# Query/key stage of a local attention: the cosine product from PSUM on VectorE, sine product and sum on GpSimd, values shifted by tile, the last norms in two parts

## The chip, the cores and the metric

The kernel runs on one core of a Trainium2 chip. The metric is the device time of one execution in microseconds (us), and the reported value is the median over runs.

## What is computed

The input x has 4 batches of 1024 tokens with 128 features. It is normalised per token, and two branches work on the result: a small attention block with a feed-forward layer (called A here), and two layers of a windowed attention with a gated feed-forward layer (B). Both are added to x. The change lies in branch B, in what stands between the projection and the attention of each layer:

```python
def _layer(x, wqkv, qs, ksc, wo, lg, lb, w1, b1, w2, b2):
    h = shift_token(x)
    q, k, v = jnp.split(h @ wqkv, 3, axis=-1)      # 8 heads of 64
    ...
    q = l2norm(q) * qs
    k = l2norm(k) * ksc
    q = q * cos * scale + rotate_half(q) * sin * scale
    k = k * cos / scale + rotate_half(k) * sin / scale
    o = local_attention(q, k, v)                   # windows of 64, each looks at itself and the one before
    x = x + o @ wo
    ...
```

The norm is a factor per head and token, so the kernel rotates first and puts the factor in later: for keys by a multiplication, for queries as the scale of the exponential.

## The kernel before, in words

One loop over the four batches holds one program per engine. The order on each engine is the order in which its function is written, and the engines meet at counting semaphores. All of q and k is kept transposed, features on partitions: 8 tiles of 128 features (two heads each), in two chunks of 512 tokens, so 16 tiles of 128x512 per layer. In each chunk k = 0 to 3 are the keys, 4 to 7 the queries. Four PSUM banks form a ring for all products (`product`, L510); a product waits for `drained`, the bank's release by its last reader.

The stage around the change, per tile:
- TensorE makes the product (L510) in a ring bank.
- ScalarE copies it with the q or k scale into `raw` (L976, four slots) and its square into `sq` (L980), which releases the bank.
- SP sends two DMAs that exchange rows of `raw` pairwise into `rot` (L452, four slots).
- VectorE makes `pc` = raw x cosine table (L1038) and `ps_` = rot x sine table (L1040), two buffers each (`rotate`).
- GpSimd adds them into `qk` (L494). VectorE's next use of a buffer waits for the sum two tiles before.

After four tiles TensorE sums the squares over the heads (`sum_squares`, L739). After the 8 tiles of a chunk come four value products, which ScalarE copies into `vB` (L995); the sums of squares are copied (L990) and transposed (`turn_sums`, L747), and VectorE takes the inverse root of them in small steps (`norms`, L292 to L297) and splits those of the keys into three bf16 parts (L1176 to L1179). The parts are transposed (L755), copied (L965) and spread over the partitions by a product; VectorE multiplies the keys by them (`scale`, L1188). The norms of chunk 0 are taken at the start of chunk 1, those of chunk 1 after its last tile. In layer 0 ScalarE also has the logarithm and exponential of branch A's layer norm there (`ln_root`, L921 and L926), right after chunk 0.

The values are needed shifted by 64 tokens as well: SP copies each chunk of `vB` with two DMAs into `vS` (L460, L462) once all its four tiles are there.

The window attention then takes 8 tiles of 128 queries: mask (L620) and scores (L628), maxima (L1085), exponentials by ScalarE (L872), their scaling by VectorE (L1103) and GpSimd (L500), transposes (L640), products with the values (L656). ScalarE's and VectorE's functions for it are called `window_attention` too.

## Time and profile before

| What | Value |
|---|---|
| Median of 3 runs | 1446.84 us (1443.94 to 1450.88) |
| The profiled execution, its own time | 1459.8 us |
| Span in that profile | 1458.1 us |
| Mean granted TensorE clock | 0.877 |
| Busy: TensorE, VectorE, ScalarE, GpSimd | 1124.0, 878.6, 768.9, 291.5 us |
| GpSimd sums `qk<-pc,ps_` (L494) | 128 of 1518 ns mean |
| Sine products `ps_<-rot,tab_s` (L1040) | 128 of 1347 ns mean |
| Cosine products `pc<-raw,tab_s` (L1038) | 128 of 854 ns mean |

The span is the time from the first to the last instruction of the profiled execution; the execution's own time has what lies around it. A mean mixes steps that ran alone with steps that had to wait for another engine inside their own duration, so single rows of the time line say more than the means here.

### The profile page before, as it was taken

Reading aid. Unit: us, or ns where it says so; the run is one execution under the profiler, and the core shown is the slowest. Engines: PE = TensorE matmul, PEld = TensorE weight load, DVE = VectorE, ACT = ScalarE, POOL = GpSimd, SP = SyncE. Lnnn points to the kernel's source line nnn. Section 1 sums busy time; section 2 is a strip of 40 time slices with the busy share of each in tenths; the row PEclk is TensorE's granted clock in tenths of the full one; section 3 lists DMA queues with packets and bytes.
Section 4 is the critical chain, followed back from the end, with each engine's and each line's share of the span. In section 5 each row is a group of like instructions: output and inputs, shape, how many; then the busy total and the mean of one; then the engine's idle time right before and its main releaser. Section 6 shows DMA issues by size and latency. Waiting matters only on the chain. (4 is left out here: it accounts for less than half of the span.)

```text
span 1458.1 us, 23509 instructions
## 1 busy us (share of the span) xinstructions
PE 1124.0 (77%) x8682; PEld 620.1 (43%) x8754; DVE 878.6 (60%) x1738; ACT 768.9 (53%) x1928; POOL 291.5 (20%) x228
## 2 busy tenths in 40 slices
PE   5986788678698668867869877886787976797677
PEld 4752453154374245325437425432534732542353
DVE  5549655963445865596345596468545467648744
ACT  1355674485235556447523556653942453945574
POOL 1105112410101411241010141033202033204210
PEclk9698899889859879988986988997997796999799
DMA  6003101400101310140010131023001014003100
GB/s 260 1 29 117 27 1 58 112 2 15 31 1 45 101 27 1 58 112 2 15 32 1 51 98 23 1 73 98 2 15 32 1 59 111 2 1 123 48 16 15
DMA packets 39201, 66.22 MB, mean 45 GB/s; under 512 B 5408, under 2 KB 19232, under 8 KB 37152
## 3 DMA queue, kind: packets, MB, share of 16 engines
q1 hardware_dynamic: 37920, 62.43, 14.0%
q10 hardware_dynamic: 1152, 2.10, 0.4%
q8 instruction: 78, 1.28, 0.4%
q14 instruction: 51, 0.42, 0.1%
HBM read 13.12 MB, written 2.10 MB: 10 GB/s over the span
## 5 line engine op out<-in xcount | busy, mean ns | idle before, releaser
L494 POOL TENSOR_TENSOR qk<-pc,ps_ 128x512 f32<-128x512 f32 x128 | 194.3, 1518 | 583.8 <-DVE ps_ L1040 583.8
L872 ACT ACTIVATE prob<-bank,negb,inv_norm 128x128 f32<-128x128 f32 x512 | 233.0, 580 | 57.3 <-DVE negb L1087 57.3
L1040 DVE TENSOR_TENSOR ps_<-rot,tab_s 128x512 f32<-128x512 f32 x128 | 172.5, 1347 | 25.9 <-DMA rot<-raw 25.9
L872 ACT ACTIVATION_READ_ACCUMULATOR prob<-bank,negb,inv_norm 128x1 f32 x512 | 163.3, 328 | 0.0
L510 PE MATMUL bank<-hTz,wb_s 128*128 128x512 f32 x256 | 139.5, 675 | 4.3 <-ACT sq L980 4.3
L1085 DVE TENSOR_REDUCE negb<-bank 128x8 f32<-128x1024 f32 x64 | 78.3, 1223 | 94.5 <-PE bank L628 94.4
L976 ACT ACTIVATE raw<-bank,vec_s 128x512 f32<-128x512 f32 x128 | 90.0, 703 | 81.6 <-PE bank L510 46.5
L500 POOL TENSOR_TENSOR prob<-prob,recb 128x512 f32<-128x512 f32 x64 | 66.7, 1041 | 320.1 <-DVE recb L1107 320.1
L1038 DVE TENSOR_TENSOR pc<-raw,tab_s 128x512 f32<-128x512 f32 x128 | 109.3, 854 | 18.2 <-ACT raw L976 18.1
L656 PE MATMUL bank<-probT,vS 128*64 128x64 f32 x1024 | 67.9, 231 | 38.6 <-issue 34.2
L510 PE MATMUL bank<-hTz,w_s 128*128 128x512 f32 (+1 forms) x192 | 87.8, 602 | 12.2 <-DVE hTz L1127 12.2
L620 PE MATMUL bank<-cbf_s 128*128 128x512 bf16 x80 | 35.7, 485 | 71.8 <-ACT prob L872 56.0
L980 ACT ACTIVATE sq<-bank 128x512 f32<-128x512 f32 x128 | 77.8, 608 | 24.1 <-PE bank L739 24.1
L536 PEld LDWEIGHTS bank<-kD,qZ 32*128 32x128 f32 x1024 | 81.7, 245 | 20.2 <-issue 20.2
L841 ACT ACTIVATE a_probT<-bank 128x512 f32<-128x512 f32 x64 | 38.1, 596 | 92.9 <-PE bank L547 92.9
L536 PE MATMUL bank<-kD,qZ 32*128 32x64 f32 (+1 forms) x1024 | 86.9, 335 | 0.0
L628 PE MATMUL bank<-qk 64*64 64x128 f32 (+1 forms) x2048 | 86.5, 311 | 0.0
L628 PEld LDWEIGHTS bank<-qk 64*64 64x64 f32 x2048 | 68.5, 158 | 37.0 <-issue 37.0
L1051 DVE TENSOR_REDUCE a_max<-bank 128x8 f32<-128x512 f32 x64 | 43.9, 686 | 64.5 <-PE bank L536 64.5
L510 PE MATMUL bank<-wb_s,hTz 128*128 128x512 f32 x128 | 75.6, 693 | 3.6 <-ACT sq L980 3.4
L510 PEld LDWEIGHTS bank<-hTz,wb_s 128*128 128x128 f32 x256 | 49.5, 208 | 65.6 <-issue 58.0
L656 PEld LDWEIGHTS bank<-probT,vS 128*64 128x64 f32 x1024 | 55.7, 140 | 50.8 <-issue 42.9
(151 smaller groups left out, 2020.8 us busy)
## 6 DMA issues: line engine op xcount, KB each, us to landing
rot<-raw SPq DMA_DIRECT2D x256, 128.0 KB, 2.0
vS<-vB SPq DMA_DIRECT2D x24, 512.0 KB, 4.4
vS<-vB SPq DMA_DIRECT2D x8, 384.0 KB, 5.7
xn_tok<-x SPq DMA_DIRECT2D x5, 512.0 KB, 3.6
tab_s<-tabs SPq DMA_DIRECT2D x1, 2048.0 KB, 21.0
vS<-x SPq DMA_DIRECT2D x4, 512.0 KB, 3.7
out<-vS SPq DMA_DIRECT2D x8, 256.0 KB, 2.4
wb_s<-wb SPq DMA_DIRECT2D x1, 1536.0 KB, 16.6
```

The costliest lines, as they stand in the source:

```text
L494: pool.tensor_tensor(dst, pc[:, j % 2, :], ps_[:, j % 2, :], ALU.add).then_inc(sum_rdy, 1)
L500: pool.tensor_tensor(p, p, wide(recb[:, t % 2, 1, :]), ALU.mult).then_inc(win_norm[1], 1)
L510: mm = pe.matmul(bank[0:m, i % RING, 0:n], lhs, rhs, start=(q == 0), stop=(q == len(parts) - 1))
L536: mm = pe.matmul(bank[:, m % 4, n0:(w + 1) * 2 * A_WIN], qZ[r, q0 // A_WIN, :, :].rearrange("p j q -> p (j q)"), kD[r, k0:q0 + A_WIN], sta ...
L628: mm = pe.matmul(dst[64 * half:64 * half + 64, g, (h + 1) * P - w:(h + 1) * P], qk[r, h, q0:q0 + 64], qk[r, 4 + h, q0 + 64 - w:q0 + 64], s ...
L656: mm = pe.matmul(head_bank[t % 2][64 * g:64 * g + 64, h * P + 64 * half:h * P + 64 * half + 64], v, probT[:, t % 2, g, h, 64 * half:64 * h ...
L872: ins = act.activation(prob[:, t % 2, g, h, :], s_bank[t % 2][:, g, h * P:(h + 1) * P], ACT.Exp, bias=negb[:, t % 2, g, h:h + 1], scale=qu ...
L976: act.activation(raw[:, jb % 4, :], bank[:, i % RING, :], ACT.Identity, scale=vec_s[:, g:g + 1]).then_inc(raw_rdy, 1)
L980: act.activation(sq[:, jb % 4, :], bank[:, i % RING, :], ACT.Square)\
L1038: dve.tensor_tensor(pc[:, j % 2, :], raw[:, jb % 4, :], ct, ALU.mult)
L1040: dve.tensor_tensor(ps_[:, j % 2, :], rot[:, jb % 4, :], st, ALU.mult).then_inc(prod_rdy, 1)
L1085: link(dve.tensor_reduce(b_, s_bank[t % 2].rearrange("p g (h k) -> p g h k", h=4), AX_X, ALU.max, negate=True))
```

## The change

- VectorE makes the cosine product straight from the product's PSUM bank, the q or k scale included, in one instruction after ScalarE has made the square, and this releases the bank.
- GpSimd makes the sine product (`exchanged`) and the sum. The product of a tile is issued ahead of the sum of the tile before it.
- ScalarE's copy into `raw` waits for the exchange that last read the slot. A new semaphore `squared` says that a square is there.
- The sums of squares of chunk 1 are turned in two parts, keys (n = 1) and queries (n = 2); the norms of the queries of chunk 1 are taken inside the attention, ahead of the third tile's maxima.
- The values are shifted tile by tile in chunk 1, tiles 0 to 3 behind the exchanges of its first four tiles, tiles 4 to 7 at its end; each tile has its own semaphore.
- The scores of the tiles 0 to 3 wait for the sums of chunk 0, those of the tiles 4 to 7 for chunk 1; `prob` lies over `sq`, and `probT` over `raw`, so the first copy into `probT` waits for the last sum.

```diff
-        with nc.sbuf_tensor("prob", [P, 2, 2, 4, P], F32) as prob, nc.sbuf_tensor("probT", [P, 2, 2, 4, P], F32) as probT:
+        with nc.sbuf_tensor("probT", [P, 2, 2, 4, P], F32) as probT:
             pass
         raw = sb("raw", [P, 4, CH])
         rot = sb("rot", [P, 4, CH])
...
+        with nc.sbuf_tensor("prob", [P, 2, 2, 4, P], F32) as prob:
+            pass
         sq = sb("sq", [P, 4, CH])
...
                             sp.wait_ge(prod_rdy, jb - 3)
                         for r in range(2):
                             sp.dma_start(rot[r::2, slot, :], raw[1 - r::2, slot, :]).then_inc(rot_rdy[slot], 16)
-                        if jb % B_QK == B_QK - 1:
...
+                        if jb // B_QK % CHUNKS:
+                            k = jb % B_QK
+                            for t in range(TPC, TILES) if k == B_QK - 1 else (k,) if k < TPC else ():
                                 taken(sp, values_use(l, t))
-                            if l:
-                                sp.wait_ge(win_heads, on(l, 0))
-                            t0, t1 = c * TPC, (c + 1) * TPC
-                            sp.dma_start(vS[64:128, t0:t1, :], vB[0:64, t0:t1, :]).then_inc(v_shifted, 16)
-                            u1 = min(t1, TILES - 1)
-                            sp.dma_start(vS[0:64, t0 + 1:u1 + 1, :], vB[64:128, t0:u1, :]).then_inc(v_shifted, 16)
+                                if t == TPC:
+                                    sp.wait_ge(sums_turned, 3 * l + 3)
+                                if l:
+                                    sp.wait_ge(win_heads, on(l, 0))
+                                sp.dma_start(vS[64:128, t, :], vB[0:64, t, :]).then_inc(v_shifted[t], 16)
+                                if t + 1 < TILES:
+                                    sp.dma_start(vS[0:64, t + 1, :], vB[64:128, t, :]).then_inc(v_shifted[t + 1], 16)
...
                 def _(pool):
+                    def exchanged(l, c, k):
...
+                        j = pair(l, c, k)
+                        jb = j - 4
+                        pool.wait_ge(rot_rdy[jb % 4], 32 * (jb // 4 + 1))
+                        pool.wait_ge(sum_rdy, j - 1)
+                        pool.tensor_tensor(ps_[:, j % 2, :], rot[:, jb % 4, :],
+                                           tab_s[:, 3 if k < 4 else 1, cc(c)], ALU.mult).then_inc(prod_rdy, 1)
...
-                                else:
-                                    pool.wait_ge(prod_rdy, j - 4 + 1)
-                                    dst = qk[:, qk_tile(k), cc(c)]
...
+                                    pool.tensor_tensor(dst, pc[:, j % 2, :], ps_[:, j % 2, :],
...
+                                if c == 0 and k == 0:
...
+                                        pool.wait_ge(mm_full, USE0["a_wo"] + 4)
+                                        pool.wait_ge(tab_b_in, 16)
+                                    exchanged(br, 0, 0)
+                                if k + 1 < B_QK or c + 1 < CHUNKS:
+                                    exchanged(br, c + (k + 1) // B_QK, (k + 1) % B_QK)
+                                pool.wait_ge(prod_rdy, j - 4 + 1)
+                                taken(pool, qk_use(br, c, k))
+                                pool.tensor_tensor(qk[:, qk_tile(k), cc(c)], pc[:, j % 2, :], ps_[:, j % 2, :],
                                                    ALU.add).then_inc(sum_rdy, 1)
...
+                        if t % TPC == 0:
+                            pe.wait_ge(sum_rdy, pair(l, t // TPC, B_QK - 1) + 1)
...
-                        pe.wait_ge(v_shifted, 32 * (l * CHUNKS + t // TPC + 1))
+                        pe.wait_ge(v_shifted[t], (32 if t else 16) * (l + 1))
...
                                 k = 4 * part + m
-                                taken(pe, qk_use(l, c, k))
-                                mm = pe.matmul(bank[32 * m:32 * m + 32, 4 + c, :], sum_s[:, part, :], sq[:, m, :],
...
+                                pe.wait_ge(squared, pair(l, c, k) - 3)
+                                alone = c == 1
+                                mm = pe.matmul(bank[32 * m:32 * m + 32, 4 + (c and not part), :], sum_s[:, part, :],
+                                               sq[:, m, :], start=(alone or part == 0), stop=(alone or part == 1),
+                                               skip_group_check=True)
                             mm.then_inc(ss_done, 1)
...
-                        def turn_sums(c):
...
+                            pe.wait_ge(sums_copied, l * 3 + n + 1)
...
-                                if tt == 0:
+                                if c == 0 and tt == 0:
                                     sum_squares(c, 1)
-                                if tt == 1:
-                                    turn_sums(c)
+                                if c == 0 and tt == 1:
+                                    turn_sums(0)
+                                if c and tt == 0:
+                                    turn_sums(1)
+                                if c and tt == 1:
+                                    sum_squares(c, 1)
+                        turn_sums(2)
                         turn_norms(1)
...
-                                    act.wait_ge(prod_rdy, jb - 3)
...
-                                act.activation(sq[:, jb % 4, :], bank[:, i % RING, :], ACT.Square)\
-                                   .then_inc(drained[i % RING], 1)
+                                act.activation(sq[:, jb % 4, :], bank[:, i % RING, :], ACT.Square).then_inc(squared, 1)
                                 if c and k == 3:
...
+                            if c:
+                                copy_sums(1)
...
-                                if tt == 0:
-                                    act.wait_ge(ss_done, (l * CHUNKS + c + 1) * 2)
-                                    act.activation(ss[:, c, :], bank[:, 4 + c, :], ACT.Copy)\
-                                       .then_inc(sums_copied, 1)
+                                if c == 0 and tt == 0:
+                                    copy_sums(0)
+                                if c and tt == 2:
+                                    copy_sums(2)
...
-                            jb = j - 4
-                            dve.wait_ge(raw_rdy, RAW0[br] + c * 8 + k + 1)
-                            dve.tensor_tensor(pc[:, j % 2, :], raw[:, jb % 4, :], ct, ALU.mult)
-                            dve.wait_ge(rot_rdy[jb % 4], 32 * (jb // 4 + 1))
-                            dve.tensor_tensor(ps_[:, j % 2, :], rot[:, jb % 4, :], st, ALU.mult).then_inc(prod_rdy, 1)
+                            qs = V_L + br * VL_N + VL_QS + qk_tile(k) // 4
+                            dve.wait_ge(squared, j - 3)
+                            dve.scalar_tensor_tensor(pc[:, j % 2, :], bank[:, i % RING, :], vec_s[:, qs:qs + 1], ct,
+                                                     ALU.mult, ALU.mult).then_inc(drained[i % RING], 1)
...
+                        if t == 0:
+                            dve.wait_ge(sum_rdy, pair(l, 1, B_QK - 1) + 1)
...
-                    def window_attention(l):
...
                         for t in range(TILES):
+                            if t == 1:
+                                norms(2)
...
-                        def norms(c):
-
...
+                        def norms(n):
...
+                            dve.wait_ge(sums_turned, l * 3 + n + 1)
+                            c, e0, e1 = ((0, 0, 4), (1, 0, 2), (1, 2, 4))[n]
+                            y = inv_norm[:, c, :, :, e0:e1].rearrange("p t k e -> p (t k) e")
+                            inv_root(dve, link, bank[:, 4 + n, :].rearrange("p (t e) -> p t e", e=32)[:, :, e0:e1],
+                                     1e-24, ALU.max, 16 * (e1 - e0), y)
+                            if n == 2:
+                                return
...
-                        for k in range(4, B_QK):
-                            dve.wait_ge(sum_rdy, pair(l, 1, k) + 1)
                         scale(1, range(4))
-                        window_attention(l)
```

GpSimd's order at the start of the query/key stage of layer 0, before (`qk<-pc,ps_` is the sum, `prob<-prob,recb` the scaling in the attention, `rotary_products` the semaphore of the two products):

```order
L494 TENSOR_TENSOR qk<-pc,ps_ 128x512 [waits product_ready,rotary_products]
L494 TENSOR_TENSOR qk<-pc,ps_ 128x512 [waits rotary_products] x15
L500 TENSOR_TENSOR prob<-prob,recb 128x512 [waits window_sums_inverted] x8
```

and now, first the start of the stage, then its end (`rows_exchanged` is the exchange, `rotated` the sum's semaphore; the bank's release stands for the cosine product):

```order
L483 TENSOR_TENSOR ps_<-rot,tab_s 128x512 [waits rows_exchanged0,rotated,rotation_tables_b_loaded,product_ready]
L483 TENSOR_TENSOR ps_<-rot,tab_s 128x512 [waits rotated,rows_exchanged1]
L514 TENSOR_TENSOR qk<-pc,ps_ 128x512 [waits bank2_drained,rotary_products]
L483 TENSOR_TENSOR ps_<-rot,tab_s 128x512 [waits rotated,rows_exchanged2]
L514 TENSOR_TENSOR qk<-pc,ps_ 128x512 [waits bank3_drained,rotary_products]
L483 TENSOR_TENSOR ps_<-rot,tab_s 128x512 [waits rotated,rows_exchanged3]
L514 TENSOR_TENSOR qk<-pc,ps_ 128x512 [waits bank0_drained,rotary_products]
...
L483 TENSOR_TENSOR ps_<-rot,tab_s 128x512 [waits rotated,rows_exchanged3]
L514 TENSOR_TENSOR qk<-pc,ps_ 128x512 [waits bank0_drained,rotary_products]
L514 TENSOR_TENSOR qk<-pc,ps_ 128x512 [waits bank2_drained,rotary_products]
L520 TENSOR_TENSOR prob<-prob,recb 128x512 [waits window_sums_inverted] x8
```

GpSimd has two steps per tile in place of one, and the product for the next tile stands ahead of each sum.

VectorE's order in the attention of layer 0, from the scaling of the first tile to the maxima of the third, before:

```order
L1101 RECIPROCAL recb<-sumb 128x4 [waits window_probs_ready]
L1103 TENSOR_TENSOR prob<-prob,recb 128x512 [waits vector_step]
L1107 RECIPROCAL recb<-sumb 128x4 [waits window_probs_ready]
L1085 TENSOR_REDUCE negb<-bank 128x8 [waits window_probs_ready,window_scores_ready]
L1087 TENSOR_TENSOR negb<-negb,inv_norm 128x8 [waits vector_step]
```

and now:

```order
L1139 RECIPROCAL recb<-sumb 128x4 [waits window_probs_ready]
L1141 TENSOR_TENSOR prob<-prob,recb 128x512 [waits vector_step]
L1145 RECIPROCAL recb<-sumb 128x4 [waits window_probs_ready]
L295 TENSOR_SCALAR nw<-bank 128x32 [waits sums_of_squares_turned]
L296 TENSOR_SCALAR inv_norm<-nw 128x16x2 [waits vector_step]
L298 TENSOR_TENSOR nw<-inv_norm 128x32 [waits vector_step]
L299 SCALAR_TENSOR_TENSOR nw<-nw 128x32 [waits vector_step]
...
L300 SCALAR_TENSOR_TENSOR inv_norm<-nw,inv_norm 128x16x2 [waits vector_step]
L1121 TENSOR_REDUCE negb<-bank 128x8 [waits window_probs_ready,window_scores_ready,vector_step]
L1123 TENSOR_TENSOR negb<-negb,inv_norm 128x8 [waits vector_step]
```

The inverse root of the queries of chunk 1, eleven small steps of 128x32, has come in ahead of the third tile's maxima (L1121).

## Rows read from the trace of the kernel before

**Rows 1.** The page, part 1: busy time, share of the span, instructions of each engine.
```profile
PE 1124.0 (77%) x8682; PEld 620.1 (43%) x8754; DVE 878.6 (60%) x1738; ACT 768.9 (53%) x1928; POOL 291.5 (20%) x228
```

**Rows 2.** Time line, TensorE: first mask product of two window attentions; start us, length us, engine.
```profile
1236.81 0.63 PE L620 MATMUL bank<-cbf_s 128*128 128x512 bf16 x1 [1.87 <-DVE qk L1188]
...
1370.53 0.63 PE L620 MATMUL bank<-cbf_s 128*128 128x512 bf16 x1 [2.32 <-DVE qk L1188]
```

**Rows 3.** Time line, VectorE, layers 0 and 1 of the last batch.
```profile
1184.56 0.69 DVE L1040 TENSOR_TENSOR ps_<-rot,tab_s 128x512 f32<-128x512 f32 x1 [1.85 <-DMA rot<-raw]
...
1321.99 0.69 DVE L1040 TENSOR_TENSOR ps_<-rot,tab_s 128x512 f32<-128x512 f32 x1 [1.84 <-DMA rot<-raw]
1322.60 0.69 DVE L1038 TENSOR_TENSOR pc<-raw,tab_s 128x512 f32<-128x512 f32 x1
...
1327.17 0.68 DVE L1038 TENSOR_TENSOR pc<-raw,tab_s 128x512 f32<-128x512 f32 x1
1327.78 1.75 DVE L1040 TENSOR_TENSOR ps_<-rot,tab_s 128x512 f32<-128x512 f32 x1
```

**Rows 4.** Time line, GpSimd: set-up, first batch, layer 1 of the last batch.
```profile
0.75 0.52 POOL L345 MEMSET vS<- 64x512 f32 x1 [0.29 <-POOLq L1397]
1.21 0.09 POOL L346 MEMSET xT<- 128x1 f32 x1
...
27.04 1.81 POOL L473 MEMSET vS<- 128x2048 f32 x1 [25.64 <-POOLq L323]
28.90 0.49 POOL L476 MEMSET vS<- 64x64 f32 x2
35.48 1.27 POOL L494 TENSOR_TENSOR kD<-pc,ps_ 128x512 f32<-128x512 f32 x1 [6.09 <-DVE ps_ L1032]
...
1327.33 1.65 POOL L494 TENSOR_TENSOR qk<-pc,ps_ 128x512 f32<-128x512 f32 x1 [0.63 <-DVE ps_ L1040]
...
1361.34 1.27 POOL L494 TENSOR_TENSOR qk<-pc,ps_ 128x512 f32<-128x512 f32 x1 [1.23 <-DVE ps_ L1040]
1378.51 1.04 POOL L500 TENSOR_TENSOR prob<-prob,recb 128x512 f32<-128x512 f32 x1 [15.90 <-DVE recb L1107]
```

**Rows 5.** Time line, VectorE: steps that run beside a GpSimd step.
```profile
36.27 0.75 DVE L1032 SCALAR_TENSOR_TENSOR ps_<-bank,bias,tab_s 128x512 f32<-128x512 f32 x1
...
1351.20 0.68 DVE L1188 TENSOR_TENSOR qk<-bank,qk 128x512 f32<-128x512 f32 x1
1351.80 1.37 DVE L1038 TENSOR_TENSOR pc<-raw,tab_s 128x512 f32<-128x512 f32 x1
```

**Rows 6.** Time line, TensorE: six products at full clock, one at the lower.
```profile
1317.58 5.31 PE L510 MATMUL bank<-hTz,wb_s 128*128 128x512 f32 x12
...
1355.02 2.07 PE L510 MATMUL bank<-wb_s,hTz 128*128 128x512 f32 x2
```

**Rows 7.** Time line, ScalarE: logarithm, exponential (layer 0), first raw copy (layer 1).
```profile
1193.38 1.28 ACT L921 ACT_TABLE_LOAD   x1
...
1197.25 1.15 ACT L926 ACTIVATE oT<-oT 128x512 f32<-128x512 f32 x2
...
1318.64 0.69 ACT L976 ACTIVATE raw<-bank,vec_s 128x512 f32<-128x512 f32 x1 [4.82 <-PE bank L510]
```

**Rows 8.** Time line, VectorE: the last norms of layer 1.
```profile
1361.73 0.93 DVE L293 TENSOR_SCALAR inv_norm<-nw 128x64 int32<-128x64 int32 x1
1362.69 0.23 DVE L295 TENSOR_TENSOR nw<-inv_norm 128x64 f32<-128x64 f32 x1
...
1365.68 0.19 DVE L1179 TENSOR_TENSOR rsp<-nw,rsp 128x32 bf16<-128x32 f32 x1
```

**Rows 9.** Time line, VectorE: maxima of the third tile in the attention.
```profile
1381.29 1.22 DVE L1085 TENSOR_REDUCE negb<-bank 128x8 f32<-128x1024 f32 x1 [2.86 <-PE bank L628]
```

**Rows 10.** Windows: us, busy PE, PEld, DVE, ACT, POOL; then granted clock, DMA share, GB/s.
```profile
1354.00:1358.00 4.00, 3.48 (x11) 0.80 (x11) 4.00 (x5) 0.66 (x2) 2.38 (x2) 0.51 0.18 66
```

**Rows 11.** Time line, SP queue: one issue of a value shift.
```profile
1336.40 0.60 SPq L462 DMA_DIRECT2D vS<-vB  x1
```

More of the change, by code:

```diff
@@ L206, in program @@
         next_in = sem("next_x_loaded")
-        v_shifted = sem("values_shifted")
+        v_shifted = [sem(f"values_shifted{t}") for t in range(TILES)]
         win_scored = sem("window_scores_ready")
@@ L289, in inv_root @@
             if root is not None:
-                v, t, s = (z.rearrange("p (a e) -> p a e", e=4) for z in (v, t, s))
+                v, t, s = (z.rearrange("p (a e) -> p a e", e=root.shape[-1]) for z in (v, t, s))
                 y = root
@@ L880, in window_lay @@
                         act.wait_ge(win_turned, 2 * on(l, t) + 2)
+                        if t == 0:
+                            act.wait_ge(sum_rdy, pair(l, 1, B_QK - 1) + 1)
                         if on(l, t) >= 2:
@@ L962, in _, with copy_sums @@
                     for l in range(LAYERS):
+                        def copy_sums(n):
+                            act.wait_ge(ss_done, l * 4 + n + 2)
+                            act.activation(ss[:, n % 2, :], bank[:, 4 + n % 2, :], ACT.Copy).then_inc(sums_copied, 1)
                         def copy_norms(c):
@@ L1201, in _ @@
                         norms(1)
[L1202 to L1203 removed]
                         scale(1, range(4))
[L1205 removed]
+                        window_attention(l, norms)
                         for c in range(CHUNKS):
```

27 lines of the change are left out of this document (12 added, 15 removed).

## Prediction

> **What bounds the kernel now.** I read the page first, then the time lines of VectorE (DVE) and GpSimd (POOL) through the query/key stage, then that of ScalarE, and TensorE's clock by windows. The page names no single engine: TensorE is busy 77%, VectorE 60% [rows 1]. The change touches one stage, which runs eight times (four batches, two layers), so that stage is what must be read. I let it begin at the first sine product, which waits for the exchanged rows, and end at the first mask product of the window attention (PE L620): 1321.99 to 1370.53 us, 48.5 us, in layer 1 of the last batch, and 1184.56 to 1236.81, 52.3 us, in layer 0 [rows 2, 3].
>
> In it VectorE never rests: cosine product, sine product, next tile, and three tile starts lie 4.57 us apart, 2.28 a tile. But a sine product takes 1.75 us, and 0.69 where GpSimd is idle [rows 3]. The GpSimd sum beside it takes 1.65 us with VectorE's two-tensor products around it and 1.27 without [rows 4]. The two engines take turns whenever VectorE reads two SBUF tensors: the sine product really starts when the sum ends. What reads PSUM is free of this: a scaling step takes 0.68 us beside a sum, the two-tensor product right behind it stretches to 1.37, and the very form that the change brings (PSUM, a column, a table) took 0.75 us beside a sum of 1.27 [rows 4, 5].
>
> **What the change does to it.** VectorE keeps one product per tile, 0.75 us, instead of two; GpSimd gets the other beside its sum. VectorE's saving (1.5 us a tile) is worth nothing by itself once GpSimd is slower than it.
>
> *GpSimd's pair.* A step over three full SBUF tiles takes 1.27 us undisturbed; the only other GpSimd form of this size, with a broadcast operand, takes 1.04. A step that waits for its own engine's last result starts 0.05 us after its end; one that doesn't, 0.06 before it [rows 4]. A pair is 1.21 + 1.27 + 0.05 = 2.5 us, with bounds 2.1 (both at 1.04) and 2.6 (nothing hidden). I take 2.5, since the product reads two full tiles just as the sum does. The product is issued one tile ahead of its sum.
>
> *The path in layer 1*, from the same start: the first product 1.2, six pairs to the sum of tile 5: 16.2. Here the stage has a knot. There are two pc buffers, so tile 7's cosine product (0.75) waits for the sum of tile 5; its bank is what the fourth value product wants (0.9); then come tile 8's own product (0.9 [rows 6]), the raw copy 0.7, issue and exchange 2.7 (1319.33 to 1321.99 [rows 3, 7]) and three hops of 0.1: 22.4. GpSimd is out of work at 18.7 and waits 3.7 us. Before, VectorE filled this time with the first norms, so what is gained by an engine that has no norms to do is lost again. Then the sum of tile 7 comes at 24.9, seven more pairs end at 42.4, the last sum at 43.7.
>
> *The last norms* are next on VectorE after tile 15's cosine product, at 40.7, with three GpSimd steps still to run. All their small steps but the first read SBUF only: before, the second took 0.93 us instead of some 0.2, until the last sum (1361.34 + 1.27) was over [rows 4, 8]. Three are held so up to 43.7; eleven are left, at 0.245 each (13 of them lie between 1362.69 and 1365.87): 46.4. From there to the mask product it is 4.66 us as before [rows 2, 8]: 51.1. Against 48.5 that is **+2.5 us**.
>
> *Layer 0.* ScalarE's logarithm and exponential (5.0 us from 1193.38 on) stand ahead of the value copies [rows 7]. In the new order their input is ready at 12.9 and they end at 17.9, the copies run to 20.9, and tile 8's rows come at 24.3, 1.9 later than in layer 1. That makes 53.0 against 52.3: **+0.7**.
>
> *Norms inside the attention.* Eleven steps of 0.245, 2.7 us, plus up to 1.0 held by GpSimd's scaling at 1378.51 [rows 4], go into a gap of VectorE of 2.86 us [rows 9]. They make the third tile's maxima some 0.7 us late: +0.6 a stage (0 to 1.6).
>
> *Clock.* TensorE's granted clock was 0.51 (towards 1.2 GHz) in part of the second half, after stretches with little to do; a product took 2.07 us there, 0.89 at full clock (2.4 GHz) [rows 6, 10]. The knot has two products on the path. The bounds are 0 and +2.3, with another 1.1 at the end; I take +0.5, since before this place ran at full clock.
>
> *The rest.* Starting the scores on the first half's sums gains nothing while the norms of the second half's keys end last. The shifts by tile cost SP some 0.6 us an issue [rows 11]: four issues, 2.4 us a tile in four tiles, still under a pair. Tile 8's exchange no longer stands behind 1 MB of shifted values, but is late for other reasons. Probabilities that lie over the squares, and the raw copy's wait for the exchange instead of the product, cost nothing: both are over before.
>
> **Sum:** 4 x 2.5 + 4 x 0.7 + 8 x 0.6 + 8 x 0.5 = 21.6, +22 us. On the profiled execution (1459.8 us, some 13 above the median of the three runs) that is 1482; carried to the median of 1446.8 it is **1469 us**.
>
> A rule beside it. A lone step takes 1.27 us [rows 4]. The Trainium skill (GPSIMD Engine Reference, 3.1 Elementwise — side-by-side cycle accounting) gives about 2.6 cycles per element for a two-input step at 1.2 GHz, by estimate 1.11 us for 512, the rest being dispatch; with the dispatch hidden a pair would be 2.3 and the time that of rival 3. Its 4.1 Engine selection sends elementwise work to VectorE and so speaks against the change; the rows agree for a single step, 0.69 against 1.27 us.
>
> **Rivals.**
> (1) *GpSimd's pairs run at 2.1 us*, as the 1.04 bounds them. The knot is then at 19.8; four tiles behind it are paced by SP at 2.5, and the last sum comes at 39.2. Layer 1 gains 1.9 us, layer 0 3.7, less 1.1 for the last two terms: 8 x 1.7 = 14, **1433**. It decides from below 2.3 us a pair. For it: 1.27 is known of additions only. Against: the new step has no broadcast operand. 0.15.
> (2) *VectorE's small steps slip in* between and beside GpSimd's. The last norms end at 44.3, 2.1 earlier, and 22 - 17 is left: **1452**. Against it stand rows 8. 0.13.
> (3) *GpSimd hides its start-up* from step to step: a pair of 2.3 saves 0.2 on the 14 pairs of the path, 22 us in all: **1447**. The rows show 0.06 hidden and no more. 0.09.
> (4) *The clock stays low* from the knot on, as TensorE has one product to do in 2.5 us: both bounds of that term, 2.9 us more a stage: **1492**. Against: the density was hardly higher before. 0.13.
> The order of instructions shows that the change does what it says, so that it does nothing is no rival.
>
> **How the numbers follow.** The forecast has 0.50; alone it would range from 1456 to 1482 (pairs of 2.4 to 2.6, the norms' 0 to 1.6). A measurement can tell 0.5%, 7 us, from no change. Slower by more: 0.50 + 0.13 = 0.63; within it: 0.13 + 0.09 = 0.22; faster: 0.15. The range from 1430 to 1490 leaves out about half of (1) and of (4) and a little of the forecast.
>
> **What would show it.** Right: ps_<-rot,tab_s on GpSimd at 1.2 to 1.3 us and pairs 2.5 apart; one GpSimd wait of 3 to 6 us a stage, for an exchange, at tile 8; pc at 0.75 us from PSUM; steps of the last norms of about 1.2 us, three times a stage; a stage of 51 us in layer 1 and 53 in layer 0. Wrong: pairs under 2.3, last norms with all steps at 0.2, GpSimd waiting for pc, or a stage that begins or ends otherwise.

## The result, and the profile after

The changed kernel takes 1502.2 us (median of 4 runs, 1498.1 to 1505.5), the kernel before in the same session 1448.9 (4 runs, 1443.9 to 1459.5): ratio 1.036, interval 1.029 to 1.042. It is slower, as forecast, but by 53 us and not by 22, and it lies outside the range (1430 to 1490). In every comparison below, the ratio leaves out runs more than 1.5% above the fastest of their kernel, while the medians are over all runs.

The first rows are the page of the changed kernel: part 1, and the groups of part 5 for the sine product, the cosine product and the sum (busy time, mean ns of one, idle time ahead and its releaser).

```profile
PE 1172.0 (78%) x8714; PEld 636.7 (42%) x8786; DVE 746.4 (50%) x1698; ACT 773.0 (51%) x1936; POOL 417.6 (28%) x356
...
L483 POOL TENSOR_TENSOR ps_<-rot,tab_s 128x512 f32<-128x512 f32 x128 | 162.2, 1270 | 509.2 <-issue 188.4
...
L1075 DVE SCALAR_TENSOR_TENSOR pc<-bank,vec_s,tab_s 128x512 f32<-128x512 f32 x128 | 96.0, 750 | 239.0 <-POOL qk L514 190.9
...
L514 POOL TENSOR_TENSOR qk<-pc,ps_ 128x512 f32<-128x512 f32 x128 | 163.4, 1280 | 0.0
```

Against [rows 1], VectorE has lost 132 us of work and GpSimd has gained 126, and VectorE now stands idle 191 us for the sums of GpSimd. The step durations are those of the prediction: 1.27 and 0.75 us.

Next is the time line of GpSimd, layer 1 of the last batch, from the first products to the last sum (start us, length us, engine):

```profile
1361.27 2.51 POOL L483 TENSOR_TENSOR ps_<-rot,tab_s 128x512 f32<-128x512 f32 x2 [48.00 <-issue]
1363.74 1.27 POOL L514 TENSOR_TENSOR qk<-pc,ps_ 128x512 f32<-128x512 f32 x1
1365.15 1.27 POOL L483 TENSOR_TENSOR ps_<-rot,tab_s 128x512 f32<-128x512 f32 x1
1366.37 1.26 POOL L514 TENSOR_TENSOR qk<-pc,ps_ 128x512 f32<-128x512 f32 x1
1367.78 1.27 POOL L483 TENSOR_TENSOR ps_<-rot,tab_s 128x512 f32<-128x512 f32 x1
...
1384.36 1.27 POOL L483 TENSOR_TENSOR ps_<-rot,tab_s 128x512 f32<-128x512 f32 x1 [3.55 <-DMA rot<-raw]
...
1395.35 1.27 POOL L483 TENSOR_TENSOR ps_<-rot,tab_s 128x512 f32<-128x512 f32 x1 [0.61 <-DMA rot<-raw]
...
1398.13 1.28 POOL L483 TENSOR_TENSOR ps_<-rot,tab_s 128x512 f32<-128x512 f32 x1 [0.28 <-DMA rot<-raw]
...
1401.26 1.27 POOL L483 TENSOR_TENSOR ps_<-rot,tab_s 128x512 f32<-128x512 f32 x1 [0.63 <-DMA rot<-raw]
...
1404.18 1.27 POOL L483 TENSOR_TENSOR ps_<-rot,tab_s 128x512 f32<-128x512 f32 x1 [0.43 <-ACT vB L1032]
1405.41 2.50 POOL L514 TENSOR_TENSOR qk<-pc,ps_ 128x512 f32<-128x512 f32 x2
```

Three things are to be seen. A pair (product and sum, GpSimd's work for one tile) takes 2.63 us (1365.15 to 1367.78): the sum starts 1.22 behind its product, the next product 1.41 behind the sum. The knot, where GpSimd runs out of work, stands at the ninth tile, as forecast (3.55 us for an exchange). And four more waits follow, which the forecast didn't have. In the same place of layer 0 the knot is longer:

```profile
1242.32 1.26 POOL L483 TENSOR_TENSOR ps_<-rot,tab_s 128x512 f32<-128x512 f32 x1 [6.79 <-DMA rot<-raw]
```

By windows, TensorE's granted clock around the knot of layer 0 and in the second half of layer 1 (columns as in [rows 10], which has 0.51 over 4 us of the second half before; 0.5 is the level of 1.2 GHz):

```profile
1228.00:1236.00 8.00, 7.40 (x16) 2.06 (x17) 4.28 (x4) 4.46 (x8) 7.25 (x6) 0.55 0.01 2
...
1389.00:1405.00 16.00, 13.23 (x24) 3.90 (x25) 7.40 (x12) 5.10 (x9) 13.76 (x12) 0.50 0.38 116
```

The last norms of layer 1 came as forecast, three small steps held until GpSimd's last sum is over, and then free (to compare with [rows 8]):

```profile
1404.67 0.82 DVE L296 TENSOR_SCALAR inv_norm<-nw 128x32 int32<-128x32 int32 x1
1405.52 1.21 DVE L298 TENSOR_TENSOR nw<-inv_norm 128x32 f32<-128x32 f32 x1
1406.77 1.19 DVE L299 SCALAR_TENSOR_TENSOR nw<-nw 128x32 f32<-128x32 f32 x1
1407.99 0.19 DVE L300 SCALAR_TENSOR_TENSOR inv_norm<-nw,inv_norm 128x32 f32<-128x32 f32 x1
```

**Where the time went.** From the first sine product to the first mask product, as the prediction measures it, the eight stages take 407.0 us before and 443.6 after: +36.6, in layer 1 48.9 on average and +5.0 each, in layer 0 52.9 and +4.2 each. The attention behind them, from the first mask product to the end of the last product with the values, takes 354.8 and 359.8 (+5.0). The other 3.6 us of the 45.0 between the two profiled executions (1459.8 and 1504.8) lie ahead of the first stage, which begins at 106.1 us before and at 109.7 after. The change leaves that stretch alone, and it takes 100 to 110 us in the traces of this study, whatever the kernel. The step from 45 to the 53 of the medians is no work of the kernel: the profiled execution of before lay 11 us above its runs' median, that of after 3.

### The profile page after: what moved, and what is told of

The parts are those of the page before. It is cut to its first block and busy times, and to the rows that moved or that the text cites. A ratio compares the mean times of both kernels' runs of the same rounds, so it can differ in the third digit from the quotient of the medians.

```text
span 1503.1 us, 24013 instructions
## 1 busy us (share of the span) xinstructions
PE 1172.0 (78%) x8714; PEld 636.7 (42%) x8786; DVE 746.4 (50%) x1698; ACT 773.0 (51%) x1936; POOL 417.6 (28%) x356
## 5 line engine op out<-in xcount | busy, mean ns | idle before, releaser
L483 POOL TENSOR_TENSOR ps_<-rot,tab_s 128x512 f32<-128x512 f32 x128 | 162.2, 1270 | 509.2 <-issue 188.4
L1075 DVE SCALAR_TENSOR_TENSOR pc<-bank,vec_s,tab_s 128x512 f32<-128x512 f32 x128 | 96.0, 750 | 239.0 <-POOL qk L514 190.9
L530 PE MATMUL bank<-hTz,wb_s 128*128 128x512 f32 x256 | 156.6, 739 | 60.7 <-DVE pc L1075 60.6
L514 POOL TENSOR_TENSOR qk<-pc,ps_ 128x512 f32<-128x512 f32 x128 | 163.4, 1280 | 0.0
L1121 DVE TENSOR_REDUCE negb<-bank 128x8 f32<-128x1024 f32 x64 | 78.2, 1223 | 72.8 <-PE bank L650 72.5
L530 PE MATMUL bank<-wb_s,hTz 128*128 128x512 f32 x128 | 90.0, 807 | 12.4 <-DVE pc L1075 12.4
L662 PE MATMUL bank<-ident_s,prob 128*128 128x128 f32 x512 | 81.2, 307 | 0.5 <-POOL prob L520 0.2
L678 PEld LDWEIGHTS bank<-probT,vS 128*64 128x64 f32 x1024 | 56.9, 143 | 51.1 <-issue 42.2
```

The source lines that it names most:

```text
L483: pool.tensor_tensor(ps_[:, j % 2, :], rot[:, jb % 4, :], tab_s[:, 3 if k < 4 else 1, cc(c)], ALU.mult).then_inc(prod_rdy, 1)
L514: pool.tensor_tensor(qk[:, qk_tile(k), cc(c)], pc[:, j % 2, :], ps_[:, j % 2, :], ALU.add).then_inc(sum_rdy, 1)
L530: mm = pe.matmul(bank[0:m, i % RING, 0:n], lhs, rhs, start=(q == 0), stop=(q == len(parts) - 1))
L662: mm = pe.transpose(turn_bank[g][:, h * P:(h + 1) * P], prob[:, t % 2, g, h, :], ident_s[:, :])
L678: mm = pe.matmul(head_bank[t % 2][64 * g:64 * g + 64, h * P + 64 * half:h * P + 64 * half + 64], v, probT[:, t % 2, g, h, 64 * half:64 * h ...
L1075: dve.scalar_tensor_tensor(pc[:, j % 2, :], bank[:, i % RING, :], vec_s[:, qs:qs + 1], ct, ALU.mult, ALU.mult).then_inc(drained[i % RING], 1)
```

## The experiments

Below, "stage" runs from VectorE's first cosine product to the first mask product, in the last batch (layer 0, layer 1), since the sine product moves between engines: 54.8 and 51.1 us before, 59.4 and 56.0 in the changed kernel. Ratios are against the kernel before on the same chip. Its median there was 1452.2 us for experiments 1 to 4, 1453.7 for 5 to 8 and 1455.9 for 9 to 12 (1448.9 beside the changed kernel), so a difference in us between two groups is uncertain by some 5 us. Line numbers in rows are those of each experiment's own kernel. The experiments stand in the order of the argument, not of their numbers.

**1. The sine product goes back to VectorE.** On the changed kernel, in VectorE's rotate and (the lines taken out) in GpSimd's program:

```diff
-                    def exchanged(l, c, k):
...
-                                if k + 1 < B_QK or c + 1 < CHUNKS:
-                                    exchanged(br, c + (k + 1) // B_QK, (k + 1) % B_QK)
...
+                            jb = j - 4
+                            dve.wait_ge(rot_rdy[jb % 4], 32 * (jb // 4 + 1))
+                            dve.tensor_tensor(ps_[:, j % 2, :], rot[:, jb % 4, :], st, ALU.mult).then_inc(prod_rdy, 1)
```

> The changed kernel with the sine product back on VectorE (cosine product still from PSUM, GpSimd again only adds; split norms, value shift by tile and the buffers as in the change). If GpSimd's pair of 2.63 us a tile is what made the stages long, the tile now costs GpSimd's sum 1.27 and VectorE's sine product 0.65 behind it, near 2.0 us, 0.3 less than the 2.28 of the kernel before: stages of 49 to 52 us, and 1405 to 1445 us in all. If instead the split norms, the shift by tile or the bank held until the square cost the time, most of the 53 us stays: 1480 us or more.

Measured: 1422.4 us, ratio 0.978 (0.969 to 0.986); stages 50.0 and 47.8. Time line of VectorE and one sum of GpSimd, layer 1, just behind the stage's start (first half):

```profile
1287.97 0.74 DVE L1062 SCALAR_TENSOR_TENSOR pc<-bank,vec_s,tab_s 128x512 f32<-128x512 f32 x1
1288.13 1.28 POOL L501 TENSOR_TENSOR qk<-pc,ps_ 128x512 f32<-128x512 f32 x1 [0.63 <-DVE ps_ L1066]
1288.63 1.32 DVE L1066 TENSOR_TENSOR ps_<-rot,tab_s 128x512 f32<-128x512 f32 x1
1289.88 0.74 DVE L1062 SCALAR_TENSOR_TENSOR pc<-bank,vec_s,tab_s 128x512 f32<-128x512 f32 x1
```

A tile takes 1.91 us (1287.97 to 1289.88): the cosine product keeps its 0.74 us beside GpSimd's sum, and only the sine product takes turns with it. It stretches to 1.32 us and ends 0.54 behind the sum. One move, the sine product to GpSimd, thus costs 80 us by the medians (1502 against 1422). Of the 82 us between the two profiled executions 71 lie in the eight stages (461.1 against 390.3) and 10 ahead of the first, which the edit doesn't touch, so the move itself costs 70 to 80 us. The rest of the change together makes the kernel some 30 us faster than before. That is the main answer. Which part of the rest brings the 30 us, the next runs ask.

**2. The cosine product from PSUM, alone on the kernel before:**

```diff
-                            dve.wait_ge(raw_rdy, RAW0[br] + c * 8 + k + 1)
-                            dve.tensor_tensor(pc[:, j % 2, :], raw[:, jb % 4, :], ct, ALU.mult)
+                            qs = V_L + br * VL_N + VL_QS + qk_tile(k) // 4
+                            dve.wait_ge(squared, j - 3)
+                            dve.scalar_tensor_tensor(pc[:, j % 2, :], bank[:, i % RING, :], vec_s[:, qs:qs + 1], ct,
+                                                     ALU.mult, ALU.mult).then_inc(drained[i % RING], 1)
```

(ScalarE's square signals squared instead of drained, and TensorE's sums of squares wait for that.)

> The kernel before with one part of the change alone: the cosine product is read from PSUM (VectorE releases the bank behind the square), the sine product stays on VectorE, norms and value shift as before. By the pair of ports the tile goes from 2.28 to about 2.0 us, 16 tiles a stage and 8 stages, less what a late transfer or the end of the stage gives back: 1405 to 1440 us. If the bank that is held longer holds TensorE up at the knot, nothing is won: 1450 us or more. Against the run with split norms it tells what the norms, the shift by tile and the buffers are worth by themselves: within 10 us of it if they cost nothing.

Measured: 1450.8 us, ratio 1.000 (0.996 to 1.004); stages 53.0 and 51.1. The expectation of a gain failed, though the tile falls to 1.9 us in the first half here too. VectorE at the ninth tile in layer 0:

```profile
1206.92 0.74 DVE L1039 SCALAR_TENSOR_TENSOR pc<-bank,vec_s,tab_s 128x512 f32<-128x512 f32 x1
1212.62 0.69 DVE L1042 TENSOR_TENSOR ps_<-rot,tab_s 128x512 f32<-128x512 f32 x1 [4.96 <-DMA rot<-raw]
```

In layer 1 the same wait is 3.01 us. What eight tiles won, one exchange takes back. It is issued behind the value shift of the first half. The issues of that stretch (KB each, median us from issue to landing):

```profile
rot<-raw SPq DMA_DIRECT2D x10, 128.0 KB, 2.1
vS<-vB SPq DMA_DIRECT2D x2, 512.0 KB, 5.4
```

**7. Experiment 1 with the value shift by half again:**

```diff
-                        if jb // B_QK % CHUNKS:
-                            k = jb % B_QK
-                            for t in range(TPC, TILES) if k == B_QK - 1 else (k,) if k < TPC else ():
...
+                        if jb % B_QK == B_QK - 1:
+                            c = jb // B_QK % CHUNKS
+                            for t in range(c * TPC, (c + 1) * TPC):
                                 taken(sp, values_use(l, t))
...
+                            sp.dma_start(vS[64:128, t0:t1, :], vB[0:64, t0:t1, :]).then_inc(v_shifted[0], 16)
```

> The first experiment (sine product on VectorE, 1422 us) with the value shift by half instead of by tile, as in the kernel before. In the second experiment's trace VectorE waits 4.96 us for the exchange of the ninth tile, behind a value shift of 512 KB in two transfers (5.4 us from issue to landing); in the first experiment this wait is gone. If that transfer is the cause, 3 to 5 us come back a stage: 1442 to 1455 us. If the wait went for another reason (the split sums, the order of the squares), 1422 us stay. The prediction priced the shift by tile at nothing.

Measured: 1458.1 us median of ten runs, ratio 0.995 (0.989 to 1.001); stages 52.5 and 51.0. Its ten runs scatter from 1429 to 1465 (the ratio counts four of them, with a median of 1444.4), so the shift by tile is worth 22 to 36 us here. That the wait is back is plain: it has the length that it has in experiment 2. VectorE at the ninth tile, layer 1, and the same place of experiment 1:

```profile
1343.49 0.74 DVE L1063 SCALAR_TENSOR_TENSOR pc<-bank,vec_s,tab_s 128x512 f32<-128x512 f32 x1
1347.25 0.69 DVE L1067 TENSOR_TENSOR ps_<-rot,tab_s 128x512 f32<-128x512 f32 x1 [3.02 <-DMA rot<-raw]
```

```profile
1303.99 0.75 DVE L1062 SCALAR_TENSOR_TENSOR pc<-bank,vec_s,tab_s 128x512 f32<-128x512 f32 x1
1304.65 0.68 DVE L1066 TENSOR_TENSOR ps_<-rot,tab_s 128x512 f32<-128x512 f32 x1
```

**9. The value shift by tile, alone on the kernel before** (the same lines of SP and TensorE as in the change, but for the count of the semaphore of the turned sums).

> The kernel before with the value shift by tile alone (cosine product from SBUF, sine product on VectorE, norms as before). VectorE's wait of 1.93 us for the exchange of the ninth tile in layer 0, and what stands for it in layer 1, lie behind the shift of 512 KB; the GpSimd wait at the ninth tile is 10.0 us in layer 0 and 5.8 in layer 1, the norms' steps of 3.7 us (and 2.4 of the layer norm in layer 0) stay. If the shift is the cause there as in the run with the sine product on VectorE, 1.5 to 3 us a stage go: 1425 to 1442 us. If the shift only weighs where the cosine product comes from PSUM, 1450 us stay.

Measured: 1455.3 us, ratio 1.003 (0.999 to 1.006); stages 52.7 and 51.4. In layer 0 VectorE's wait of 1.93 us at the ninth tile is gone and the stage 2.1 us shorter; the whole time shows nothing that can be measured. So neither part is worth anything alone. With the cosine product from PSUM in place, the shift by tile is worth most of the 30 us (experiment 1 against 7). The change's other parts (norms in two pieces, the raw copy's wait for the exchange, the earlier scores) bring little: 0.995 with them in experiment 7 against 1.000 without them in experiment 2. The two parts alone together on the kernel before were not run. With a tile of 2.28 us VectorE comes to the ninth tile when its exchange has landed (layer 1) or nearly so (layer 0); with 1.91 it comes 3 us earlier, and only then the large transfer ahead of the exchange is on the path in both layers. This is a constraint that moved, and two parts of one change that can't be priced one at a time.

**3. Four buffers for the sine products** in the changed kernel:

```diff
-        ps_ = sb("ps_", [P, 2, CH])
+        ps_ = sb("ps_", [P, 4, CH])
...
-                        pool.wait_ge(sum_rdy, j - 1)
-                        pool.tensor_tensor(ps_[:, j % 2, :], rot[:, jb % 4, :],
+                        pool.wait_ge(sum_rdy, j - 3)
+                        pool.tensor_tensor(ps_[:, j % 4, :], rot[:, jb % 4, :],
```

> The changed kernel with four buffers for the sine products instead of two, so that GpSimd's product waits for a sum three instructions back and no more for the one right before it. If the 0.15 us idle ahead of each product is the semaphore of its own last sum, it goes, and with it 0.13 to 0.2 us x 14 tiles x 8 stages: 15 to 22 us less, 1480 to 1487 us. If it is the price of starting a GpSimd instruction of this kind, the gap stays and the time too: 1502 us.

Measured: 1488.9 us, ratio 1.027 (1.023 to 1.032), 13 us less than the change; stages 57.5 and 55.6. GpSimd, first half of layer 1:

```profile
1345.94 1.27 POOL L483 TENSOR_TENSOR ps_<-rot,tab_s 128x512 f32<-128x512 f32 x1
1347.17 1.26 POOL L514 TENSOR_TENSOR qk<-pc,ps_ 128x512 f32<-128x512 f32 x1
1348.39 1.26 POOL L483 TENSOR_TENSOR ps_<-rot,tab_s 128x512 f32<-128x512 f32 x1
```

The gap is gone: 1.22 from sum to product in place of 1.41, a pair of 2.44. The waits for exchanges in the second half grow in return (1.07 and 1.45 us there), which is why 13 us come and not 20.

**4. Four buffers for the cosine products** instead:

```diff
-        pc = sb("pc", [P, 2, CH])
+        pc = sb("pc", [P, 4, CH])
...
-                        if j >= 2:
-                            dve.wait_ge(sum_rdy, j - 1)
+                        n_ = 2 if A else 4
+                        if j >= n_:
+                            dve.wait_ge(sum_rdy, j - n_ + 1)
```

> The changed kernel with four buffers for the cosine products instead of two, all else as in the change. If the wait at the ninth tile (3.55 us in layer 1, 6.79 in layer 0) comes from the cosine product that waits for a buffer and holds the bank of the value product, it shrinks to under 1 us in layer 1 and to about 3 in layer 0 (where the low clock and the split of the logarithms stay): 20 to 40 us less, 1462 to 1482 us. If TensorE's low clock or the exchange sets it, the wait stays and the time too.

Measured: 1461.3 us, ratio 1.008 (1.005 to 1.011), 41 us less than the change; stages 52.9 and 51.8. GpSimd's wait at the ninth tile is gone in layer 1 (a sum waits 1.07 us for its cosine product instead) and 1.9 us long in layer 0. The four late waits are gone too in this last batch (layer 1 of two other batches keeps one, of 1.1 us). But VectorE's first norms, 5.0 us in the changed kernel, now take 11.7 (layer 1):

```profile
1329.39 0.21 DVE L295 TENSOR_SCALAR nw<-bank 128x64 f32<-128x64 f32 x1
...
1331.69 1.17 DVE L300 SCALAR_TENSOR_TENSOR inv_norm<-nw,inv_norm 128x64 f32<-128x64 f32 x1
1332.90 1.19 DVE L298 TENSOR_TENSOR nw<-inv_norm 128x64 f32<-128x64 f32 x1
...
1340.86 0.19 DVE L1223 TENSOR_TENSOR rsp<-nw,rsp 128x32 bf16<-128x32 f32 x1
1340.96 2.72 DVE L1076 SCALAR_TENSOR_TENSOR pc<-bank,vec_s,tab_s 128x512 f32<-128x512 f32 x4
```

GpSimd hardly rests, and eight of the fifteen small steps wait out a step of GpSimd (1.14 to 1.22 us in place of some 0.2). The knot was bad for GpSimd and good for the norms.

**10. Both together,** four cosine and three sine buffers.

> The changed kernel (both products and the sum as in the change) with four buffers for the cosine products and three for the sine products. The one alone took 41 us, the other 13. If the knot and GpSimd's wait for its own last sum are separate terms they add: 1440 to 1455 us, equal to the kernel before, and GpSimd's pair of 2.44 us x 16 = 39 us a stage is what is left. If the one was the cover of the other, 1458 us or more.

Measured: 1462.8 us, ratio 1.006 (1.002 to 1.010); stages 52.8 and 51.1. The terms don't add: a pair is 2.44 us and the time that of experiment 4. The sum now meets a late cosine product (GpSimd, layer 1), which stands behind the norms on VectorE, where eight small steps in a row are held:

```profile
1350.28 1.26 POOL L514 TENSOR_TENSOR qk<-pc,ps_ 128x512 f32<-128x512 f32 x1 [2.03 <-DVE pc L1076]
```

```profile
1343.48 1.19 DVE L299 SCALAR_TENSOR_TENSOR nw<-nw 128x64 f32<-128x64 f32 x1
1344.70 1.18 DVE L300 SCALAR_TENSOR_TENSOR inv_norm<-nw,inv_norm 128x64 f32<-128x64 f32 x1
1345.92 1.19 DVE L298 TENSOR_TENSOR nw<-inv_norm 128x64 f32<-128x64 f32 x1
```

With the sine product on GpSimd, no choice of buffers tried here was faster than the kernel before.

**5. Filler products for the clock** in the changed kernel; they compute nothing that is used:

```diff
                                 product(u, [(wb_s[:, l, at:at + P], hT[:, cc(c)])])
+                                if c:
+                                    for _ in range(3):
+                                        pe.matmul(bank[:, 7, :], identb, wmask[0], start=True, stop=True)
```

> The changed kernel with three bf16 filler products of 128x512 into a bank that the stage doesn't read, behind each query/key product of the second half; they add no result. If TensorE's clock of 0.50 from the thirteenth tile on makes the last exchanges late (1.3 us of waits a stage, and products of 2.07 us in place of about 1.1), the clock stays at 1.0 there, these waits shrink to under 0.3 and the last sum comes 1 to 2 us earlier a stage: 1486 to 1496 us. If the exchanges are late for another reason (the order of the releases of banks), the waits stay and the fillers cost what they take: 1502 us or more.

Measured: 1504.5 us, ratio 1.036 (1.028 to 1.044), no gain. The fillers lifted the clock (third-to-last column) to 0.89 over the same 16 us of layer 1 in which the changed kernel had 0.50, and the late waits did not shrink. Two are left there, of 0.63 and 2.27 us, against four of 1.95 in all in the changed kernel:

```profile
1389.00:1405.00 16.00, 11.89 (x40) 3.88 (x43) 6.33 (x9) 5.54 (x11) 12.67 (x11) 0.89 0.44 134
```

```profile
1403.91 1.27 POOL L483 TENSOR_TENSOR ps_<-rot,tab_s 128x512 f32<-128x512 f32 x1 [2.27 <-DMA rot<-raw]
```

This speaks against the clock as the main cause of the late exchanges, and for the order in which banks come free. It is argued and not shown: the fillers take TensorE's time themselves, and experiment 4, which took the late waits away by two more buffers, raised the stage's clock as well (0.89 over layer 1's stage, 0.76 in the changed kernel). What the clock alone costs is not isolated.

**6. The last norms whole, ahead of the attention,** in the changed kernel:

```diff
-                        window_attention(l, norms)
+                        norms(2)
+                        window_attention(l)
...
-                            if t == 1:
-                                norms(2)
```

> The changed kernel with the second part of the last norms ahead of the attention instead of inside it: nothing is left out, 11 small VectorE steps stand between the first norms and the first maxima, off the mask's path, but ahead of the first maxima. Priced by the rows of the last norms, 2.2 to 3 us stand ahead of the maxima, which wait for the mask product 4.7 us behind the last sum anyway, and the attention gets back the 0.6 us a stage that it lost: between 5 us less and 10 us more than 1502. If splitting them is worth much, 15 us or more are lost.

Measured: 1496.8 us, ratio 1.031 (1.021 to 1.041); stages 59.2 and 55.9. This is within the uncertainty of the change: splitting the last norms neither costs nor brings anything that shows.

**8. A faster version: the cosine product one tile ahead.** Experiment 1 with four cosine buffers, and in VectorE's program (half(k, 0) is the cosine product of tile k, half(k, 1) its sine product):

```diff
-                                rotate(l, c, k, qk_use(l, c, k), tab_s[:, r, cc(c)], tab_s[:, r + 1, cc(c)])
...
+                                if k + 1 < B_QK:
+                                    half(k + 1, 0)
+                                half(k, 1)
+                                if c and 3 <= k < 7:
+                                    scale(0, (k - 3,))
```

> The first experiment (sine product on VectorE, 1422 us) with four buffers for the cosine products and VectorE's cosine product of the next tile ahead of the sine product of this one, so that a bank is released before VectorE stands waiting for an exchange. In the first experiment the second half waits 0.8, 1.3, 0.4, 1.2 and 0.6 us for exchanges a stage, each behind a product that waited for a bank. If the order of the releases makes them late, most of these 4 us go: 1390 to 1410 us. If TensorE's low clock makes them late, the waits stay: 1418 to 1425 us.

Measured: **1407.8 us**, ratio 0.968 (0.959 to 0.977), the fastest kernel of this study, with experiment 12; stages 46.6 and 46.3. The groups of VectorE for the sine products, in experiment 1 and here (last column: idle time ahead), show where it came from:

```profile
L1066 DVE TENSOR_TENSOR ps_<-rot,tab_s 128x512 f32<-128x512 f32 x128 | 125.4, 980 | 50.9 <-DMA rot<-raw 50.5
```

```profile
L1050 DVE TENSOR_TENSOR ps_<-rot,tab_s 128x512 f32<-128x512 f32 x128 | 133.0, 1044 | 4.6 <-DMA rot<-raw 3.9
```

51 us of waits for exchanges became 5, though 15 us came off the time, since not all of them lay on the path.

**11. Experiment 8 with the first norms behind the ninth tile.**

```diff
-                            if c:
-                                norms(0)
                             half(0, 0)
...
                                 half(k, 1)
+                                if c and k == 0:
+                                    norms(0)
```

> The eighth experiment (1408 us) with the first half's norms on VectorE behind the ninth tile's products instead of ahead of them. There GpSimd stands 5.0 us at the ninth tile in layer 1, for norms of 5 us on VectorE. If only their place costs, 1.5 to 3 us a stage go: 1385 to 1397 us. If TensorE, which waits for these norms to be transposed ahead of the thirteenth product, is late by as much as they are, nothing is won: 1405 us or more.

Measured: 1445.6 us, ratio 0.996 (0.992 to 0.999), 38 us more than experiment 8; stages 52.7 and 49.6. The rival named in the expectation held: TensorE, in program order, stands at the transposes of these norms with the next products queued behind them.

```profile
1330.60 0.60 PE L766 MATMUL bank<-cbf_s,rsp 128*24 128x128 bf16 x4 [6.09 <-DVE rsp L1215]
```

In experiment 8 the same step came after 2.67 us of idle time.

**12. Experiment 8 with the last norms whole** (the edit of experiment 6).

> The eighth experiment (1408 us) with the second part of the last norms ahead of the attention instead of inside it. In the changed kernel the same edit gave 1497 against 1502 us, no difference that the intervals can tell. If the split of the norms is worth nothing, 1400 to 1412 us again; if it is worth the 11 steps of 0.23 to 1.2 us that it takes away from before the maxima, 1420 us or more.

Measured: 1407.6 us, ratio 0.968 (0.957 to 0.980); stages 46.5 and 46.3. The same as experiment 8, so the split is worth nothing in the faster kernel either.

## Why the prediction was right in direction and wrong in size

The direction and the place of the knot were right. Two terms of the sum failed: the pair's length, and the second half, for which the forecast had no waits at all. A third, the knot in layer 0, was 2.5 us too short, and the agreement of a fourth, the norms, is luck.

- *GpSimd's pair* was forecast at 2.5 us and came at 2.63. The failed step is "a step that waits for its own engine's last result starts 0.05 us after its end": between product and sum that doesn't happen (1.22 from start to start), and behind the sum it costs 0.15. I took the 0.05 from two memsets at set-up; experiment 3 shows the true price, 0.19 a tile by taking the wait away. It is 0.13 us in each of 13 pairs, 1.7 us a stage of miss.
- *The knot* was right in place and mechanism, and experiment 4 confirms it: two cosine buffers make it, and four remove it in layer 1 and leave 1.9 of 6.8 us in layer 0. In layer 1 the ninth product came at 23.1 us of the stage, forecast 22.4; the difference is the slower pairs ahead of it. In layer 0 it came at 26.8, forecast 24.3 (6.79 us of wait). ScalarE's logarithm and exponential ended at 17.8 us of the stage, forecast 17.9; then ScalarE waited 1.31 us for the sums of squares, which took TensorE 1.94 us at a granted clock of 0.55, and 1.2 us in all for value products. The forecast had no term for that: its value copies follow without a pause.
- *The second half* is the term that was missing: "seven more pairs end at 42.4" assumed that no exchange is late once the knot is past. Four were in layer 1, 1.3 us a stage beyond the usual gap (two in layer 0, 0.9 us). Experiment 5 speaks for the release of banks by a VectorE that waits for a buffer, rather than for the clock, for which the forecast had +0.5. Which of the two it is stays open.
- These three account for layer 1: the last sum ends at 46.6 us of the stage, forecast 43.7; 0.7 by the knot, 0.9 by seven pairs, 1.3 by the late exchanges. From there all ran as forecast: three held steps, then 4.7 us to the mask product as before. The stages took 53.9 and 57.1 against 51.1 and 53.0.
- *The norms inside the attention* were forecast at +4.8 in all, and the attention is 5.0 longer, but by luck. An attention ends 43.4 to 43.7 us behind its first mask product where TensorE's granted clock is 1.00 to its end, and 45.1 to 46.2 where it has fallen. Before, three of the eight are of the longer sort, in the changed kernel five. Among the short ones the change costs 0.2 us (43.5 to 43.7), with the third tile's maxima 0.4 late, forecast 0.7. So 1 to 2 us of the 5.0 are the norms' and the rest is the clock's; why it falls in one attention and not in another, no run isolates. Experiments 6 and 12 show no gain from placing the norms elsewhere. The last 5 us of two attentions of the changed kernel (layers 0 and 1 of the last batch, 46.2 and 43.7 us long; the clock is the third number from the end):

```profile
1313.80:1318.80 5.00, 4.27 (x53) 3.78 (x49) 0.69 (x1) 1.20 (x2) 0.00 (x0) 0.50 0.01 3
1454.00:1459.00 5.00, 3.30 (x73) 2.99 (x73) 0.79 (x2) 2.06 (x4) 1.04 (x1) 1.00 0.02 5
```

- *"The rest", at nothing*, was not tried piece by piece in the changed kernel itself. With the sine product on VectorE, where a tile takes 1.91 us, the shift by tile is worth 22 to 36 us (experiments 1 and 7). There the forecast's sentence, that tile 8's exchange is freed "but is late for other reasons", is wrong; whether it is right where a tile takes 2.63 us is open.
- *The sum* was 1482 for the profiled execution; it took 1504.8. Of these 23 us 20 lie in the stages and 3.6 ahead of the first one. The other 10 are in the step to the median: the forecast took off the 13 us by which the profiled execution of before lay above its median; after, the two differ by 3. The forecast's own bounds for pair and norms, added up, give 1453 to 1488 and not 1456 to 1482; the result lies outside either.
- *The rivals.* GpSimd at 2.1 or 2.3 us a pair: no. Small steps that slip in: no, experiments 4 and 10 show them held even more often. Low clock from the knot on (1492): it happened, 0.50 over 16 us, and was the closest in time, but experiment 5 lifted the clock to 0.89 there and the time stayed, so the clock is probably not what the miss is made of.
- The Trainium skill (GPSIMD Engine Reference, 4.1 Engine selection) sends elementwise work to VectorE. This case's runs agree, and give the price: 70 to 80 us for 128 products moved (experiment 1 against the change).

## What to carry to other kernels

An engine's idle share is no measure of what it can take over: GpSimd was 20% busy, but the stage it got the work in needs its sum in every tile, and a product that costs 0.64 us in turns with it on VectorE (1.91 less the sum's 1.27) costs 1.27 to 1.41 in series on GpSimd. What paid here was to take one of the two engines' reads off the SBUF side (the cosine product from PSUM), together with whatever then becomes late next. Price the parts of a change against each other, not one by one, and look one tile ahead in program order for the step that frees a bank.

## What the runs showed of the hardware that was not expected

- A GpSimd step that waits for the semaphore of the step right before it starts 1.41 us behind that step's start; a sum that waits for its product three steps back starts 1.22 behind the step before it, and so does a product that waits for a sum five steps back (experiment 3). All last 1.27 us. That is 0.19 us a wait.
- A GpSimd without pauses starves VectorE's small steps that read SBUF. With gaps of 0.15 us eight of 15 steps take 1.1 to 1.2 us (experiment 4: 11.7 us in place of 5.0), without gaps eight in a row (experiment 10). Casts from SBUF are held as well; in the changed kernel's pauses such steps take 0.2.
- With three bf16 filler products behind each product of the second half (experiment 5) the granted clock was 0.89 over 16 us, where the changed kernel had 0.50, and the time did not change (1504.5 against 1502.2 us).
- The same attention takes some 2 us more when TensorE's granted clock falls in its last 5 us (0.50 and 46.2 us against 1.00 and 43.7). Two more of the eight being of that sort makes some 4 of the 5 us by which the attention grew.
